# Attention weights times normalised rows first, then times the value weights, with row sums from the exponentials' accumulator

## The chip, the cores and the metric

One core of one Trainium2 chip runs the whole program. The metric is the device time of one execution in microseconds, as the median over several runs. The engines are called TensorE (PE; its weight loads PEld), VectorE (DVE), ScalarE (ACT), GpSimd (POOL) and SyncE (SP, which issues DMAs here).

## What is computed

The input is 16 batches of 64 channels x 250 samples; the output is 16 x 250 x 128. Cut to what matters:

```python
h = layernorm_affine(conv3(x).T @ lin_w.T + ...)       # tokeniser, per batch 250 x 128
n = layernorm(h)                                       # n1 in the kernel
QK = (n @ Wq) @ (n @ Wk).T                             # 250 x 250 per batch
c0 = argmin(sum(QK[0], axis=1))                        # one row, found in batch 0
A  = softmax(QK / 8); A[:, c0, :] = 0
h  = h + A @ (n @ Wv)                                  # the product whose order changes
h  = h + gelu(layernorm(h) @ tril(W1).T + b1) @ tril(W2).T + b2
```

All of it is float32.

## The kernel before

The 250 tokens of a batch lie as two interleaved halves (a = 0, 1) of 125 partitions. NB is 16 batches, NP is 8 pairs of batches. Five engine programs are written out by hand and meet only through semaphores; each engine runs its own list in order, so the written order decides what can stand behind what.

Per batch b, TensorE turns the normalised rows (turn_n1, L353), multiplies them with Wq Wk^T (queries, L358) and with Wv (values, L363), makes the scores (scores, L371), turns the exponentials (turn_a, L380) and multiplies them with the values (attend, L390). The values carry a 129th column of ones, so attend also gives the softmax's row sums. Per pair, project (L400, L403) makes the tokeniser's product. A float32 product is two instructions of TensorE; a transposition here is one.

ScalarE copies every result out of PSUM (out_n1t L563, out_p L567, out_v L572, out_at L585), normalises the rows for all but the first two batches (normalize_1, L556), takes the sums of squares (squares, L547, with the accumulator), and the exponentials (exps, L578: two ACTIVATEs, one for each half).

VectorE adds the taps of the convolution (L686, L693), scales (scale_x, L703), takes statistics (stats_1 L710, aggregate_1 L716, stats_2 L765, aggregate_2 L771), the row maxima (row_max, L746) and the residual (residual, L751 reciprocal of the row sums, L753 times keep, L757 the two updates of h). For the feed-forward part it normalises (normalize_2, L893: four TENSOR_SCALARs a pair) and adds the result (finish, L883).

GpSimd takes the roots (root_x L235, root_1 L249, root_2 L263), adds beta (add_beta, L267), the first tap (L224), and b2 (add_b2, L271).

The steady part is a hardware loop (Fori) on each engine: on TensorE `queries, values, project, turn_a, scores, turn_n1, attend` for the even batch, the same without project for the odd. VectorE's loop for the pair k is

```python
residual(2 * k - 2); stats_1(k + 1); second_tap(k + 3, x_slot); aggregate_1()
third_tap(k + 3, x_slot); row_max(2 * k, 0)
stats_2(k - 1, 0); residual(2 * k - 1); stats_2(k - 1, 1); scale_x(k + 2)
row_max(2 * k + 1, 1); aggregate_2()
```

Behind the loop the last three pairs are written out, and in them the first pairs of the feed-forward part begin: normalize_2(1, 1) stands between residual(12) and row_max(14), and GpSimd's order there is root_2(NP - 3), add_b2(0), add_b2(1), root_2(NP - 2), add_b2(2), root_2(NP - 1), then add_b2(3) to add_b2(7). ScalarE's order at the end is exps(15), out_at(15), gelu(0) with its table load, and so on.

## Time and profile before

| what | us |
|---|---|
| median of 3 runs | 112.07 |
| lowest and highest run | 110.67 to 112.18 |
| the profiled execution, device time | 111.78 |
| its span, first to last instruction | 109.9 |

The profile shows one execution, whose own device time is 1.9 us more than its span. Busy times are sums over the span; what an engine waited for is told in views of their own. Times inside the trace are counted from the start of the span.

### The profile page before, as it was taken

Reading aid. Unit: us, or ns where it says so; the run is one execution under the profiler, and the core shown is the slowest. Engines: PE = TensorE matmul, PEld = TensorE weight load, DVE = VectorE, ACT = ScalarE, POOL = GpSimd, SP = SyncE. Lnnn points to the kernel's source line nnn. Section 1 sums busy time; section 2 is a strip of 40 time slices with the busy share of each in tenths; the row PEclk is TensorE's granted clock in tenths of the full one; section 3 lists DMA queues with packets and bytes.
Section 4 is the critical chain, followed back from the end, with each engine's and each line's share of the span. In section 5 each row is a group of like instructions: output and inputs, shape, how many; then the busy total and the mean of one; then the engine's idle time right before and its main releaser. Section 6 shows DMA issues by size and latency. Waiting matters only on the chain.

```text
span 109.9 us, 2404 instructions
## 1 busy us (share of the span) xinstructions
PE 96.4 (88%) x618; PEld 76.3 (69%) x618; DVE 91.2 (83%) x335; ACT 67.9 (62%) x207; POOL 59.6 (54%) x122
## 2 busy tenths in 40 slices
PE   6976978989899999999999998999799786699930
PEld 2443465868778888888888997997686663486730
DVE  2679999999999889979979789999959999994250
ACT  3132445985668888887896989797476744226400
POOL 3327687548549649758758648509309069920000
PEclk9999999999999999999999999999999999769996
DMA  2960000000010010010000000000000003026363
GB/s 57 171 243 0 0 0 3 0 6 6 0 47 0 11 35 0 4 43 0 0 0 3 0 0 0 0 6 0 0 0 0 0 0 93 18 79 186 94 173 107
DMA packets 3838, 3.80 MB, mean 35 GB/s; under 512 B 426, under 2 KB 3703, under 8 KB 3831
## 3 DMA queue, kind: packets, MB, share of 16 engines
q1 hardware_dynamic: 3557, 3.40, 11.4%
q10 hardware_dynamic: 274, 0.33, 1.3%
q8 instruction: 2, 0.03, 0.1%
q14 instruction: 5, 0.04, 0.1%
HBM read 1.68 MB, written 2.05 MB: 34 GB/s over the span
## 4 chain that ended last, share of the span: by engine, by line
DVE 39%; PE 30%; POOL 10%; issue 9%; POOLq 3%; ACT 3%; DVEq 1%; ACTq 0%
DVE n L893 7%; PE bank_o L411 6%; DVE scaled L703 5%; PE bank_s L371 4%; DVE neg_max L746 4%; POOL rstd_x L235 4%; POOL rstd L249 4%; DVE h_all L757 3%; DVE bn L710 3%; DVE rinv_keep L753 3%; PE bank_s L497 2%; DVE bn L765 2%; DVE tap L686 2%; DVE mv L771 2%; PE bank_at L505 2%
## 5 line engine op out<-in xcount | busy, mean ns | idle before, releaser
L578 ACT ACTIVATE a<-bank_s,neg_max 125x250 f32<-125x250 f32 x32 | 13.3, 467 | 8.7 <-DVE neg_max L746 8.4
L390 PE MATMUL bank_o<-v,at 125*125 125x129 f32 x128 | 17.7, 280 | 0.0
L371 PE MATMUL bank_s<-n1t,pt 128*125 128x250 f32 x64 | 16.4, 379 | 0.6 <-ACT pt L567 0.6
L390 PEld LDWEIGHTS bank_o<-v,at 125*125 125x125 f32 x128 | 15.4, 187 | 1.7 <-ACT at L585 0.9
L893 DVE TENSOR_SCALAR n<-h_all,mean,rstd 125x128 f32<-125x128 f32 x32 | 16.0, 563 | 0.0
L746 DVE TENSOR_REDUCE neg_max<-bank_s 125x2 f32<-125x500 f32 x16 | 10.7, 671 | 2.1 <-PE bank_s L371 1.9
L556 ACT ACTIVATE n<-h_all,shift,rstd 125x128 f32 (+1 forms) x28 | 12.2, 488 | 0.3 <-POOL shift L254 0.3
L267 POOL TENSOR_TENSOR h_all<-scaled,rows_sb 125x512 f32<-125x512 f32 (+1 forms) x6 | 7.6, 1274 | 8.2 <-DVE scaled L703 8.2
L371 PEld LDWEIGHTS bank_s<-n1t,pt 128*125 128x125 f32 x64 | 10.7, 187 | 1.9 <-ACT pt L567 1.2
L380 PE MATMUL bank_at<-ident,a 125*125 125x125 f32 x64 | 10.5, 286 | 1.3 <-ACT a L578 1.3
L358 PE MATMUL bank_np<-n1t,qk_w 128*128 128x250 f32 x32 | 9.6, 382 | 1.4 <-ACT n1t L563 1.0
L757 DVE SCALAR_TENSOR_TENSOR h_all<-bank_o,rinv_keep,h_all 125x128 f32<-125x128 f32 (+1 forms) x32 | 9.8, 346 | 1.3 <-DVE rinv_keep L753 0.5
L380 PEld LDWEIGHTS bank_at<-ident,a 125*125 125x125 f32 x64 | 8.3, 188 | 2.7 <-ACT a L578 2.5
L547 ACT ACTIVATE squared<-bank_x 125x128 f32<-125x128 f32 x28 | 7.7, 298 | 3.8 <-PE bank_x L403 3.8
L271 POOL TENSOR_TENSOR hb_all<-h_all,rows_sb 125x512 f32 (+1 forms) x8 | 10.1, 1283 | 0.0
L585 ACT ACTIVATE at<-bank_at 125x500 f32<-125x500 f32 x16 | 9.5, 592 | 0.9 <-PE bank_at L380 0.9
L363 PEld LDWEIGHTS bank_v<-w_sb,n1t 128*125 128x125 f32 x64 | 9.5, 187 | 0.7
L235 POOL TENSOR_TENSOR rstd_x<-var_x_eps,neg_half 125x4 f32<-125x4 f32 (+1 forms) x10 | 9.1, 909 | 1.2
L363 PE MATMUL bank_v<-w_sb,n1t 128*125 128x128 f32 x64 | 9.6, 272 | 0.0
L646 ACT ACTIVATE n2t<-bank_x 128x500 f32<-128x500 f32 x8 | 4.7, 590 | 7.6 <-PE bank_x L490 7.5
L703 DVE SCALAR_TENSOR_TENSOR scaled<-bank_x,rstd_x,rows_sb 125x128 f32<-125x128 f32 x28 | 7.9, 343 | 1.3 <-POOL rstd_x L235 1.3
L249 POOL TENSOR_TENSOR rstd<-var_eps,neg_half 125x4 f32<-125x4 f32 (+1 forms) x10 | 8.8, 884 | 0.2
(111 smaller groups left out, 203.6 us busy)
## 6 DMA issues: line engine op xcount, KB each, us to landing
out_dram<-hb_all SPq DMA_DIRECT2D x7, 224.0 KB
x_head<-x_dram SPq DMA_DIRECT2D x4, 125.0 KB, 5.5
x_slot<-x_dram SPq DMA_DIRECT2D x4, 125.0 KB, 2.0
w_sb<-weights_dram SPq DMA_DIRECT2D x1, 320.5 KB, 5.7
out_dram<-hb_all SPq DMA_DIRECT2D x2, 112.0 KB
rows_sb<-rows_dram ACTq DMA_DIRECT2D x1, 187.5 KB
out_dram<-hb_all SPq DMA_DIRECT2D x7, 26.0 KB
tok_w<-tok_dram ACTq DMA_DIRECT2D x1, 130.0 KB, 2.7
```

Of the source, the lines that this page charges most:

```text
L235: pool.tensor_tensor(rstd_x[:, tiles], var_x_eps[:, tiles], neg_half[:, tiles], ALU.pow)\
L249: pool.tensor_tensor(rstd1[:, tiles], var1_eps[:, tiles], neg_half[:, tiles], ALU.pow)\
L363: last = nc.tensor.matmul(v_ps[:, a, :], n1t[par][:, a * H:(a + 1) * H], w_v, start=True, stop=True)
L371: last = nc.tensor.matmul(s_ps[par][:, a, :], pt[par][:, a * H:(a + 1) * H], n1t[par][:, :], start=True, stop=True)
L380: last = nc.tensor.transpose(at_ps[:, c, a * H:(a + 1) * H], a_sb[par][:, a, c * H:(c + 1) * H], ident[0:H, 0:H])
L390: last = nc.tensor.matmul(o_ps[:, a, 0:DV], at_sb[par][:, c, a * H:(a + 1) * H], v_sb[par][:, c, :], start=(c == 0), stop=(c == 1))
L556: last = nc.scalar.activation(n1[par][:, a, :], h_pairs[:, pair, n * D:(n + 1) * D], ACT.Identity, bias=shift1[:, n:n + 1], scale=rstd1[:, ...
L578: last = nc.scalar.activation(a_sb[par][:, a, :], s_ps[par][:, a, :], ACT.Exp, bias=neg_max[par][:, a:a + 1])
L703: last = nc.vector.scalar_tensor_tensor(scaled[:, n, :], src[n // 2][:, n % 2, :], rstd_x[:, n:n + 1], gamma, ALU.mult, ALU.mult)
L746: nc.vector.tensor_reduce(neg_max[par][:, :], s_ps[par], AX_X, ALU.max, negate=True).then_inc(max_ready, 1)
L757: last = nc.vector.scalar_tensor_tensor(h, o_ps[:, a, 0:D], rinv_keep[:, a:a + 1], h, ALU.mult, ALU.add)
L893: last = nc.vector.tensor_scalar(n2[par][:, n, :], h_pairs[:, j, n * D:(n + 1) * D], mean2[:, j, n:n + 1], rstd2[:, j, n:n + 1], ALU.subtr ...
```

## The change

The product A (n Wv) is made as (A n) Wv. TensorE no longer makes values. A new step, mix, multiplies the normalised rows of the batch (as weights, n1) with the turned exponentials, two products of 250 columns summed in PSUM; ScalarE copies the result out (out_mix), and attend multiplies it with Wv, two products of 128 columns. n1 gets four buffers instead of two. attend(b) moves to the step of the batch b + 2.

The row sums come from the accumulator of the exponentials (`accum_out`), into four columns for a pair. VectorE inverts them once a pair (inverse_sums), multiplies with keep once a pair (drop_row), and residual only updates h. The exponentials are written as two halves with out_mix of the batch before between them. VectorE's order changes: stats_1 and aggregate_1 stand ahead of residual(2k-2), scale_x ahead of residual(2k-1), and at the end normalize_2(1, 1) ahead of residual(12). The loops of TensorE, ScalarE and VectorE over the pairs are written out.

```diff
-            def values(b, par):
-                for a in range(2):
-                    last = nc.tensor.matmul(v_ps[:, a, :], n1t[par][:, a * H:(a + 1) * H], w_v,
-                                            start=True, stop=True)
-                last.then_inc(v_mm, 1)
+            def mix(b, par):
+                pe.wait_ge(at_ready, b + 1)
+                for c in range(2):
+                    last = nc.tensor.matmul(mix_ps, n1[b % 4][:, c, :], at_sb[par][:, c, :], start=(c == 0), stop=(c == 1))
+                last.then_inc(mix_mm, 1)
...
             def attend(b, par):
-                pe.wait_ge(at_ready, b + 1)
+                pe.wait_ge(mixed_ready, b + 1)
...
                 for a in range(2):
-                    for c in range(2):
-                        last = nc.tensor.matmul(o_ps[:, a, 0:DV], at_sb[par][:, c, a * H:(a + 1) * H],
-                                                v_sb[par][:, c, :], start=(c == 0), stop=(c == 1))
+                    last = nc.tensor.matmul(o_ps[:, a, :], mixed[par][:, a * H:(a + 1) * H], w_v, start=True, stop=True)
...
+            for b in range(2, NB - 1):
+                par = b % 2
+                queries(b, par)
+                if par == 0 and b // 2 + 2 < NP:
+                    pe.wait_ge(x_scaled, b + 4)
+                    project(b // 2 + 2)
+                if b == 2:
+                    pe.wait_ge(sums_used, 1)
+                attend(b - 2, par)
+                turn_a(b - 1, 1 - par)
+                scores(b, par)
+                turn_n1(b + 1)
+                mix(b - 1, 1 - par)
...
             queries(NB - 1, 1)
-            values(NB - 1, 1)
             turn_n2(0, 0)
+            attend(NB - 3, 1)
             turn_a(NB - 2, 0)
             scores(NB - 1, 1)
             turn_n2(1, 1)
-            attend(NB - 2, 0)
+            mix(NB - 2, 0)
             pe.wait_ge(tri_ready, 2)
             up(0, 0)
+            attend(NB - 2, 0)
             turn_a(NB - 1, 1)
             up(1, 1)
-            attend(NB - 1, 1)
+            mix(NB - 1, 1)
             turn_n2(2, 0)
             down(0, 0)
+            attend(NB - 1, 1)
...
+            def exps(b, par, halves=(0, 1)):
                 act.wait_ge(max_ready, b + 1)
-                for a in range(2):
+                for a in halves:
                     last = nc.scalar.activation(a_sb[par][:, a, :], s_ps[par][:, a, :], ACT.Exp,
-                                                bias=neg_max[par][:, a:a + 1])
-                last.then_inc(exp_ready, 1)
+                                                bias=neg_max[par][:, a:a + 1],
+                                                accum_out=exp_sum[:, 2 * par + a:2 * par + a + 1])
+                if 1 in halves:
+                    last.then_inc(exp_ready, 1)
...
+            def slot(b):
+                par = b % 2
+                xs = par == 0 and b // 2 + 2 < NP
+                out_p(b, par)
+                normalize_1((b + 1) // 2, 1 - par)
                 if xs:
...
+                out_at(b - 1, 1 - par)
...
+                out_n1t(b + 1, 1 - par)
+                exps(b, par, (0,))
+                out_mix(b - 1, 1 - par)
+                exps(b, par, (1,))
...
             out_p(NB - 1, 1)
-            out_v(NB - 1, 1)
             out_n2t(0, 0)
             out_at(NB - 2, 0)
             out_n2t(1, 1)
-            exps(NB - 1, 1)
+            exps(NB - 1, 1, (0,))
+            out_mix(NB - 2, 0)
+            exps(NB - 1, 1, (1,))
             out_at(NB - 1, 1)
             gelu(0, 0)
+            out_mix(NB - 1, 1)
...
-            def residual(b):
-                dve.wait_ge(o_mm, b + 1)
-                nc.vector.reciprocal(rinv[:, :], o_ps[:, :, D]).then_inc(rinv_ready, 1)
...
+            def inverse_sums(k):
+                dve.wait_ge(exp_ready, 2 * k + 2)
+                nc.vector.reciprocal(rinv[:, :], exp_sum[:, :]).then_inc(rinv_ready, 1)
+            def drop_row(k):
+                dve.wait_ge(rinv_ready, k + 1)
+                nc.vector.tensor_tensor(rinv_keep[:, :], rinv[:, :], keep[:, :], ALU.mult).then_inc(keep_applied, 1)
+            def residual(b, k, par):
+                dve.wait_ge(keep_applied, k + 1)
                 dve.wait_ge(o_mm, b + 1)
...
-            with dve.Fori(2, NP - 3) as k:
-                residual(2 * k - 2)
+            for k in range(2, NP - 3):
                 stats_1(k + 1)
+                inverse_sums(k - 1)
                 dve.wait_ge(bn1_ready, 2 * k + 4)
                 second_tap(k + 3, x_slot)
                 aggregate_1()
+                drop_row(k - 1)
+                residual(2 * k - 2, k - 1, 0)
                 third_tap(k + 3, x_slot)
                 row_max(2 * k, 0)
                 from_scores(k)
...
             for k in range(NP - 3, NP):
-                residual(2 * k - 2)
                 if k < NP - 1:
...
                 else:
+                    inverse_sums(k - 1)
                     normalize_2(1, 1)
+                drop_row(k - 1)
+                residual(2 * k - 2, k - 1, 0)
                 row_max(2 * k, 0)
...
-            residual(NB - 2)
+            normalize_2(2, 0)
+            inverse_sums(NP - 1)
+            drop_row(NP - 1)
+            residual(NB - 2, NP - 1, 0)
             stats_2(NP - 1, 0)
-            normalize_2(2, 0)
             normalize_2(3, 1)
-            residual(NB - 1)
+            residual(NB - 1, NP - 1, 1)
```

## Rows read from the trace of the kernel before

**Rows 1.** The page, part 1: busy time of each engine, share of the span, instructions.

```profile
PE 96.4 (88%) x618; PEld 76.3 (69%) x618; DVE 91.2 (83%) x335; ACT 67.9 (62%) x207; POOL 59.6 (54%) x122
```

**Rows 2.** The chain that ended last: start, duration, piece; one TensorE step, and one project.

```profile
19.31 0.43 PE bank_x L400 x4
19.74 0.26 PE bank_x L403 x2
...
69.35 0.89 PE bank_o L390 x8
70.24 0.42 PE bank_np L358 x2
70.66 0.44 PE bank_v L363 x4
71.10 0.44 PE bank_at L380 x4
71.53 0.86 PE bank_s L371 x4
```

**Rows 3.** Timeline (start, duration, engine, line, instruction, [idle before <-releaser]): row maxima of batches 2 and 13.

```profile
28.24 0.65 DVE L746 TENSOR_REDUCE neg_max<-bank_s 125x2 f32<-125x500 f32 x1
...
72.42 0.68 DVE L746 TENSOR_REDUCE neg_max<-bank_s 125x2 f32<-125x500 f32 x1
```

**Rows 4.** Timeline, VectorE and GpSimd over one pair of the loop (45 to 53 us).

```profile
44.73 0.37 DVE L716 BATCH_NORM_AGGREGATE mv<-bn 125x2 f32<-125x6 f32 x4
...
48.41 1.13 DVE L703 SCALAR_TENSOR_TENSOR scaled<-bank_x,rstd_x,rows_sb 125x128 f32<-125x128 f32 x4 [0.32 <-POOL rstd_x L235]
...
49.79 1.27 POOL L267 TENSOR_TENSOR h_all<-scaled,rows_sb 125x512 f32 x1 [1.41 <-DVE scaled L703]
...
50.50 0.57 DVE L753 TENSOR_TENSOR rinv_keep<-rinv,keep 125x2 f32<-125x2 f32 x1
...
52.75 0.48 DVE L686 SCALAR_TENSOR_TENSOR tap<-x_slot,tok_w,tap 128x250 f32<-128x250 f32 x1
...
53.14 0.37 DVE L716 BATCH_NORM_AGGREGATE mv<-bn 125x2 f32<-125x6 f32 x4
```

**Rows 5.** Timeline: ScalarE with and without the accumulator, and from exponentials to scores.

```profile
43.49 0.39 ACT L572 ACTIVATE v<-bank_v 125x256 f32<-125x256 f32 x1
...
43.75 0.29 ACT L547 ACTIVATE squared<-bank_x 125x128 f32<-125x128 f32 x1
...
43.91 0.22 ACT L547 ACTIVATION_READ_ACCUMULATOR squared<-bank_x 125x1 f32 x1
44.00 0.30 ACT L547 ACTIVATE squared<-bank_x 125x128 f32<-125x128 f32 x1
...
46.09 0.83 ACT L578 ACTIVATE a<-bank_s,neg_max 125x250 f32<-125x250 f32 x2 [0.44 <-DVE neg_max L746]
...
46.97 0.70 PE L380 MATMUL bank_at<-ident,a 125*125 125x125 f32 x4
...
47.51 1.01 PE L371 MATMUL bank_s<-n1t,pt 128*125 128x250 f32 x4
```

**Rows 6.** Timeline, VectorE and GpSimd: normalize_2(0, 0), normalize_2(1, 1), row_max(14).

```profile
71.20 1.11 DVE L893 TENSOR_SCALAR n<-h_all,mean,rstd 125x128 f32<-125x128 f32 x4
...
73.53 0.38 DVE L771 BATCH_NORM_AGGREGATE mv<-bn 125x2 f32<-125x6 f32 x4
...
74.75 3.09 DVE L893 TENSOR_SCALAR n<-h_all,mean,rstd 125x128 f32<-125x128 f32 x4
...
75.26 2.50 POOL L271 TENSOR_TENSOR hb_all<-h_all,rows_sb 125x512 f32<-125x512 f32 x2
...
77.77 0.67 DVE L746 TENSOR_REDUCE neg_max<-bank_s 125x2 f32<-125x500 f32 x1
```

**Rows 7.** Timeline of the last batch: table load of gelu(0), the last residual.

```profile
84.13 1.28 ACT L650 ACT_TABLE_LOAD   x1
...
87.25 0.61 DVE L757 SCALAR_TENSOR_TENSOR h_all<-bank_o,rinv_keep,h_all 125x128 f32<-125x128 f32 x2
```

More of the change, by code:

```diff
@@ L451, in _ @@
             scores(1, 1)
-            turn_n1(2, 0)
-            pe.wait_ge(v_ready, 2)
+            turn_n1(2)
             pe.wait_ge(sums_diagonal, 1)
             nc.tensor.matmul(sums_ps, ones_f[:, :], sum_diag[:, :], start=True, stop=True).then_inc(sums_spread, 1)
-            pe.wait_ge(v_ones, 2)
-            attend(0, 0)
-            pe.wait_ge(sums_used, 1)
-            with pe.Fori(1, NP - 2) as k:
-                queries(2 * k, 0)
-                values(2 * k, 0)
-                pe.wait_ge(x_scaled, 2 * k + 4)
-                project(k + 2)
-                turn_a(2 * k - 1, 1)
-                scores(2 * k, 0)
-                turn_n1(2 * k + 1, 1)
-                attend(2 * k - 1, 1)
-                queries(2 * k + 1, 1)
-                values(2 * k + 1, 1)
-                turn_a(2 * k, 0)
-                scores(2 * k + 1, 1)
-                turn_n1(2 * k + 2, 0)
-                attend(2 * k, 0)
-            for b in range(NB - 4, NB - 1):
-                queries(b, b % 2)
-                values(b, b % 2)
-                turn_a(b - 1, 1 - b % 2)
-                scores(b, b % 2)
-                turn_n1(b + 1, 1 - b % 2)
-                attend(b - 1, 1 - b % 2)
+            mix(0, 0)
+            for b in range(2, NB - 1):
[11 more added lines that the diff above has]
+                mix(b - 1, 1 - par)
             def turn_n2(j, par):
@@ L585, in out_at @@
                 nc.scalar.activation(at_sb[par][:, :, :], at_ps, ACT.Copy).then_inc(at_ready, 1)
[L587 to L591 removed]
+            def slot(b):
[3 more added lines that the diff above has]
+                normalize_1((b + 1) // 2, 1 - par)
                 if xs:
[L593 removed]
+                    act.wait_ge(x_mm, b + 6)
                     squares(0)
                     squares(1)
[L596 removed]
+                out_at(b - 1, 1 - par)
                 if xs:
@@ L636, in _ @@
             out_n1t(2, 0)
-            exps(1, 1)
-            with act.Fori(1, NP - 2) as k:
-                step(k)
-            step(NP - 2, xs=False)
+            exps(1, 1, (0,))
+            out_mix(0, 0)
+            exps(1, 1, (1,))
+            for b in range(2, NB - 1):
+                slot(b)
             def out_n2t(j, par):
@@ L650, in gelu @@
                 nc.scalar.activation(g_sb[par][:, :], f1_ps[par], ACT.Gelu, bias=b1_col).then_inc(gelu_ready, 1)
-            normalize_1(NP - 1, 1)
-            out_p(NB - 2, 0)
-            out_v(NB - 2, 0)
-            out_at(NB - 3, 1)
-            out_n1t(NB - 1, 1)
-            exps(NB - 2, 0)
             out_p(NB - 1, 1)
-            out_v(NB - 1, 1)
             out_n2t(0, 0)
@@ L848, in from_scores @@
                 stats_2(k - 1, 0)
-                residual(2 * k - 1)
+                scale_x(k + 2)
+                residual(2 * k - 1, k - 1, 1)
+                row_max(2 * k + 1, 1)
                 stats_2(k - 1, 1)
-                scale_x(k + 2)
                 dve.wait_ge(bn2_ready, 2 * k)
-                row_max(2 * k + 1, 1)
                 aggregate_2()
             dve.wait_ge(keep_ready, 1)
-            residual(0)
             stats_1(2)
+            inverse_sums(0)
             dve.wait_ge(bn1_ready, 6)
```

96 lines of the change are left out of this document (38 added, 58 removed).

## Prediction, made before the changed kernel was run

> **What bounds the kernel now.** I read the page first. TensorE is busy for 88% of the span and VectorE for 83%, ScalarE for 62% [rows 1]: two engines are near full, so a saving on one of them alone gives little, and an order that makes one wait for the other costs at once. Then I read the chain that ended last, which shows TensorE's instructions back to back where it is the bound [rows 2], and the timeline of one pair of the loop [rows 4]. From aggregate to aggregate a pair takes 8.41 us (44.73 to 53.14). Inside it lies a circuit of VectorE and GpSimd: aggregate_1, GpSimd's two roots, scale_x 3.68 us later, row_max, aggregate_2, residual, stats_1, second tap, aggregate_1 again. TensorE's own work for a pair is 2 x 3.27 + 1.38 = 7.92 us: a batch without project is attend 0.89, queries 0.42, values 0.44, turn_a 0.44, scores 0.86 and 0.22 for turn_n1 (two transpositions; four take 0.44), and project is 2 x (0.43 + 0.26) [rows 2]. So TensorE has only 0.5 us of slack in 8.41.
>
> The third view is the link between two batches: row_max, the exponentials, turn_a, the next scores. Today: scores 1.01 to their end, 0.04 to VectorE, row_max 0.67, 0.03, both exponentials 0.83, 0.05, and 0.54 from turn_a's start to the start of scores [rows 3, 5], together 3.17 us. TensorE's work for a batch is 3.27, so this link is hidden with 0.1 to spare. It is the number on which the change turns.
>
> **TensorE's work.** values (0.44) and attend (0.89) go. mix is two products of 250 columns, the shape of scores: 0.86. The new attend is two products of 128 columns, the shape of values: 0.44. Sum 1.30 against 1.33: TensorE saves 0.03 us a batch, 0.5 us in all, and only where it is the bound. That the new order of the product saves columns on paper is nearly undone, since the old one has 128 and 129 columns per product and the new one 250. A batch now takes 3.24, a pair 7.86.
>
> **ScalarE's work and the link.** out_v (256 columns, 0.26 from its start to the next start) is replaced by out_mix (250 columns), at the same price. New are the reads of the accumulator. At squares the read starts 0.16 after its ACTIVATE and the next instruction 0.09 after the read; the read lasts 0.22 [rows 5]. An exponential alone takes 0.47, and the second starts 0.36 after the first (0.83 less 0.47). With reads and out_mix between the halves the link holds: 0.36 + 0.09 for the first half, 0.28 for out_mix, then 0.35 + 0.22 for the second with its read: 1.30 us instead of 0.83. From below it could be 0.83 + 0.09 = 0.92 (out_mix costs nothing, reads overlap, and the semaphore goes with the ACTIVATE); from above it is more if mix isn't ready. It should be just ready: after scores begin, turn_n1 and mix follow at 0.86 and 1.08, mix ends at about 2.1, and the first exponential's half is done at 1.01 + 0.04 + 0.67 + 0.03 + 0.45 = 2.2. I take 1.30, the sum of the nearest rows. The link becomes 3.17 + 0.47 = 3.64 us. TensorE has 3.24 of work to cover it in an odd step and 4.62 in a step with project. So an odd step becomes 3.64 long and a pair 4.63 + 3.64 = 8.27 us, against 8.41 today.
>
> **VectorE's circuit.** A pair loses one reciprocal and one multiplication by keep. That multiplication lasts 0.57 us on the loop's path, though it has two columns: it ends when GpSimd's add_beta (49.79 + 1.27 = 51.06) ends [rows 4]. drop_row now stands behind aggregate_1, where GpSimd waits for it, so it costs 0.16 there. With scale_x, residual, row_max, stats_2, aggregate_2, stats_1, reciprocal, second tap (0.39 to its follower) one after another, each by the distance of its start to its follower's on the timeline, I get 3.68 + 1.05 + 0.54 + 0.58 + 0.50 + 0.29 + 0.79 + 0.20 + 0.40 = 8.03. That is shorter than 8.27; so VectorE's gain of 0.38 a pair is real but cut to 0.14 by the link. Written-out loops: TensorE's back edge shows at most 0.1 us, inside the slack; I give it nothing of its own.
>
> **Head.** row_max(2) starts at 28.24 [rows 3]. Before it now stand both taps of x_slot (0.40 each by their starts), less the first reciprocal and its wait (0.2): 28.84. The values of the first two batches lay beside ScalarE's copies and give nothing.
>
> **Through the pairs.** row_max(10) comes four pairs later: 28.84 + 33.08 = 61.92. From there no project covers the link; row_max(13) = 61.92 + 3 x 3.64 = 72.84 (now 72.42 [rows 3]): +0.42.
>
> **normalize_2(1, 1) and the port.** Now: aggregate_2 at 73.53, four TENSOR_SCALARs from 74.75 take 3.09 us, alongside two add_b2 from 75.26 for 2.50, and row_max(14) starts at 77.77 [rows 6]. Alone a group of four takes 1.11 (71.20); so two of the four each sat through one add of 1.27. In the new order aggregate_2 is at 73.95, and inverse_sums(6) must wait for the exponentials of batch 13: 72.84 + 0.67 + 0.04 + 1.30 = 74.85. The four instructions start at 75.07, 75.34, 75.61 and 75.88; add_b2(0) comes as now 1.73 after aggregate_2, at 75.68. So only the fourth is caught (until 77.03); but then drop_row, two inputs in SBUF, is caught by add_b2(1) until 78.2, as the 0.57 row shows for its two-column form. residual 0.54, row_max(14) at 78.8: +1.05. If drop_row slipped through, it would be 77.7. What is queued behind drop_row is the residual, then row_max(14), then everything on TensorE.
>
> The Trainium skill, page "SBUF — State Buffer", section "Who interferes with whom", says the same of drop_row: a VectorE instruction with two SBUF inputs contends with a GpSimd instruction that reads SBUF, and whoever issues first holds the port for the whole instruction. By that rule the trace agrees (0.57 us for two columns), and by that page alone the sum would be this one and not the 77.7.
>
> **Last batch.** Now the last residual starts 9.48 after row_max(14) [rows 6, 7]. New, from row_max(14) = R: exponentials done R + 2.01; turn_a, scores(15), row_max(15) at R + 3.65; exponentials with out_mix(14) done R + 5.8. TensorE: mix(14) and up(0) to R + 5.59, attend(14) to 6.03, turn_a(15) to 6.6, out_at(15) to 7.25. Then the table load of 1.28 [rows 7] and gelu(0) 0.68 end at R + 9.25, and out_mix(15) stands behind them: 9.6. down(0) 0.87 starts at 9.28, so attend(15) ends at R + 10.75 and the residual comes at R + 10.8: +1.32. Today attend(15) has no copy behind the table load; this is what the new copy costs. aggregate_2 and the rest of the tail wait for it in VectorE's order.
>
> **Sum.** 0.42 + 0.63 + 1.32 = 2.4 us. The profiled execution took 111.78 (span 109.9 and 1.9 around it), so 114.2; it lies 0.3 under the median of the runs, 112.07, which is inside their spread, so I leave it. Against the median that is +1.9%; about 2% is what a measurement of this kernel can tell from no change.
>
> **Rivals.**
> *The link stays hidden (faster).* If the exponentials' link is 0.92 and not 1.30, VectorE's 8.03 rules: row_max(10) at 60.96, then 3.27 a batch: row_max(13) at 70.8. normalize_2(1, 1) then starts 0.7 after aggregate_2 and escapes the adds, drop_row sits through one: row_max(14) at 75.5, 2.3 early; the tail costs about 0.6. Time 110.1, and under 109.8 (2%) if drop_row is free too. For it: out_mix might fit in idle time (ScalarE waits 0.44 us for the row maximum). Against: it stands behind the row maximum in ScalarE's list, not ahead. It decides where the link is under 1.0 us. Chance 0.17.
> *mix is late (slower).* If mix isn't ready when the first half is done, the second half, turn_a and scores wait. I left 0.1 us. out_at stands behind out_p and normalize_1 in ScalarE's list, and the copy lasts 0.6. If each odd step and each step without project loses 0.3 more, that is nine steps, 2.7 us: 116.9. It decides from 0.1 us of delay on. Chance 0.2.
> *The port misses drop_row, or the tail has slack.* R 1.1 earlier, or attend(15) released earlier: 112.3 to 113.2. Chance 0.15.
> *The change does what the forecast says.* Chance 0.48.
>
> The range from these: 110.8 to 116.6 leaves out part of the first two. The likeliest case's own range is 113.2 to 115.2. Faster by over 2%: 0.12; within 2% (109.8 to 114.3): 0.48; slower: 0.40, half of it from the forecast's own upper side.
>
> **What would show it.** Right: row_max of odd and even batches 3.6 and 4.6 us apart in the loop; 1.3 us from the first exponential to turn_a; a wait of turn_a for the exponentials in nearly every odd step; drop_row of over 1 us near 77 us; attend(15) behind gelu(0) and out_mix. Wrong: a pair of 8.0 (the link is hidden), of over 8.5 (mix late, second exponentials waiting for mix), row_max(14) before 77.7, or pauses of no known cause in the written-out loops.

## The result and the profile after

The changed kernel takes 113.43 us (median of 5 runs, 112.69 to 117.67), the kernel before 111.76 in the runs beside it: ratio 1.0167, 95% interval 1.0109 to 1.0224. In a second measurement it was 113.69 against 112.30: 1.013 (1.0065 to 1.0195). So it is slower by 1.3 to 1.7%: both intervals lie above 1, and only the first reaches past 2%. 114.2 us had been forecast. (The ratios here are not the quotients of the medians; the two differ by up to 0.7 points.) In some executions the granted clock is low for longer and the time some per cent greater, and the first profile of the changed kernel was of such a one, so all rows below are from the second profile, of the same kernel (span 111.9 us, device time 113.6).

The page of the changed kernel, part 1, the line that answers to [rows 1]:

```profile
PE 94.1 (84%) x554; PEld 71.1 (64%) x554; DVE 85.8 (77%) x319; ACT 71.1 (64%) x239; POOL 60.0 (54%) x120
```

TensorE is busy for 2.3 us less and VectorE for 5.4 less; ScalarE has 3.2 more, and the kernel is slower. Busy time is not even a measure of the work: before, TensorE counts as busy through the whole 8.41 us of a pair, while its products, each by the distance to its follower, add up to 7.92. So busy time doesn't tell it; the waits do. The timeline of the changed kernel over one odd step, from row_max(10) to row_max(11) (start, duration, engine, line, instruction, [idle before <-releaser]):

```profile
62.30 0.68 DVE L724 TENSOR_REDUCE neg_max<-bank_s 125x2 f32<-125x500 f32 x1 [0.60 <-PE bank_s L369]
...
63.01 0.47 ACT L562 ACTIVATE a<-bank_s,neg_max 125x250 f32<-125x250 f32 x1
...
63.38 0.19 ACT L562 ACTIVATION_READ_ACCUMULATOR a<-bank_s,neg_max 125x1 f32 x1
63.47 0.37 ACT L556 ACTIVATE mixed<-bank_m 128x250 f32<-128x250 f32 x1
63.73 0.47 ACT L562 ACTIVATE a<-bank_s,neg_max 125x250 f32<-125x250 f32 x1
...
63.89 0.51 PEld L387 LDWEIGHTS bank_o<-w_sb,mixed 128*125 128x125 f32 x4 [0.54 <-ACT mixed L556]
64.08 0.21 ACT L562 ACTIVATION_READ_ACCUMULATOR a<-bank_s,neg_max 125x1 f32 x1
...
64.43 0.61 PE L378 MATMUL bank_at<-ident,a 125*125 125x125 f32 x4
...
64.88 1.01 PE L369 MATMUL bank_s<-n1t,pt 128*125 128x250 f32 x4
...
65.93 0.68 DVE L724 TENSOR_REDUCE neg_max<-bank_s 125x2 f32<-125x500 f32 x1 [0.20 <-PE bank_s L369]
```

The step is 3.63 us. In it the exponentials, both accumulator reads and out_mix between them last from 63.01 to 64.29, 1.28 us, where both exponentials took 0.83 in [rows 5]. TensorE's weight loads for attend now wait 0.54 us for out_mix, and its products start at 63.89, 0.3 us later than back to back behind the queries; in [rows 2] there is no such gap.

The timeline of the changed kernel at row_max(14), which answers to [rows 6]:

```profile
73.19 0.68 DVE L724 TENSOR_REDUCE neg_max<-bank_s 125x2 f32<-125x500 f32 x1 [0.61 <-PE bank_s L369]
...
75.21 0.18 DVE L729 RECIPROCAL rinv<-exp_sum 125x4 f32<-125x4 f32 x1 [0.54 <-ACT a L562]
...
75.31 2.08 DVE L881 TENSOR_SCALAR n<-h_all,mean,rstd 125x128 f32<-125x128 f32 x4
...
76.03 2.50 POOL L271 TENSOR_TENSOR hb_all<-h_all,rows_sb 125x512 f32<-125x512 f32 x2
...
77.30 1.25 DVE L733 TENSOR_TENSOR rinv_keep<-rinv,keep 125x4 f32<-125x4 f32 x1
...
78.58 0.61 DVE L741 SCALAR_TENSOR_TENSOR h_all<-bank_o,rinv_keep,h_all 125x128 f32<-125x128 f32 x2
79.11 0.67 DVE L724 TENSOR_REDUCE neg_max<-bank_s 125x2 f32<-125x500 f32 x1
```

drop_row, four columns wide, takes 1.25 us: it ends when the second addition of b2 ends. And the last batch, which answers to [rows 7]:

```profile
86.32 1.28 ACT L632 ACT_TABLE_LOAD   x1
...
87.62 0.68 ACT L632 ACTIVATE g<-bank_s,w_sb 128x500 f32<-128x500 f32 x1
88.19 0.37 ACT L556 ACTIVATE mixed<-bank_m 128x250 f32<-128x250 f32 x1
...
89.32 0.60 PE L387 MATMUL bank_o<-w_sb,mixed 128*125 128x128 f32 x4
...
90.03 0.61 DVE L741 SCALAR_TENSOR_TENSOR h_all<-bank_o,rinv_keep,h_all 125x128 f32<-125x128 f32 x2 [2.10 <-PE bank_o L387]
```

Where the two profiled executions part, in us (the end is that of the last addition to the output, finish):

| stretch | before | changed | difference | forecast |
|---|---|---|---|---|
| start to row_max(0) | 16.92 | 17.45 | +0.53 | 0 |
| row_max(0) to row_max(2) | 11.32 | 11.73 | +0.41 | +0.60 |
| row_max(2) to row_max(13) | 44.18 | 44.01 | -0.17 | -0.18 |
| row_max(13) to row_max(14) | 5.35 | 5.92 | +0.57 | +0.63 |
| row_max(14) to the last residual | 9.48 | 10.92 | +1.44 | +1.32 |
| last residual to the end | 18.73 | 17.95 | -0.78 | 0 |
| sum | | | +2.00 | +2.37 |

### The profile page after: what moved, and what is told of

It reads as the page before. It is cut to its first block, busy times and chain, and to the rows that moved or that the text cites. A ratio compares the mean times of both kernels' runs of the same rounds, so it can differ in the third digit from the quotient of the medians.

```text
span 116.0 us, 2145 instructions
## 1 busy us (share of the span) xinstructions
PE 99.3 (86%) x554; PEld 74.3 (64%) x554; DVE 86.0 (74%) x319; ACT 71.1 (61%) x239; POOL 59.9 (52%) x120
## 4 chain that ended last, share of the span: by engine, by line
PE 56%; DVE 14%; ACT 12%; DMA 5%; issue 4%; POOLq 2%; POOL 1%; SPq 1%; DVEq 0%; ACTq 0%
PE bank_s L369 12%; PE bank_o L387 8%; PE bank_at L378 6%; DMA w_sb<-weights_dram 5%; ACT a L562 5%; PE bank_x L396 5%; PE bank_m L362 5%; PE bank_o L407 5%; DVE neg_max L724 5%; DVE n L881 5%; PE bank_np L356 3%; PE bank_x L399 3%; PE bank_s L478 3%; PE bank_np L486 3%; ACT mixed L556 2%
## 5 line engine op out<-in xcount | busy, mean ns | idle before, releaser
L562 ACT ACTIVATE a<-bank_s,neg_max 125x250 f32<-125x250 f32 x32 | 15.0, 469 | 3.7 <-DVE neg_max L724 2.4
L362 PE MATMUL bank_m<-at,n 125*128 125x250 f32 x64 | 16.9, 388 | 0.0
L724 DVE TENSOR_REDUCE neg_max<-bank_s 125x2 f32<-125x500 f32 x16 | 10.8, 678 | 7.9 <-PE bank_s L369 7.7
L741 DVE SCALAR_TENSOR_TENSOR h_all<-bank_o,rinv_keep,h_all 125x128 f32<-125x128 f32 x32 | 9.7, 345 | 6.1 <-PE bank_o L387 6.0
L881 DVE TENSOR_SCALAR n<-h_all,mean,rstd 125x128 f32<-125x128 f32 x32 | 14.1, 502 | 0.0
L387 PE MATMUL bank_o<-w_sb,mixed 128*125 128x128 f32 x64 | 10.9, 294 | 3.0 <-ACT mixed L556 2.0
L387 PEld LDWEIGHTS bank_o<-w_sb,mixed 128*125 128x125 f32 x64 | 8.3, 188 | 6.9 <-ACT mixed L556 6.9
L362 PEld LDWEIGHTS bank_m<-at,n 125*128 125x128 f32 x64 | 11.5, 199 | 1.5 <-ACT at L571 0.6
L540 ACT ACTIVATE n<-h_all,shift,rstd 125x128 f32<-125x128 f32 x28 | 12.4, 504 | 0.0
L407 PE MATMUL bank_o<-warm 128*64 128x512 bf16 x24 | 10.1, 587 | 1.0 <-DVE warm L759 1.0
L547 ACT ACTIVATE n1t<-bank_np 128x250 f32<-128x250 f32 x16 | 6.1, 382 | 7.9 <-PE bank_np L351 7.9
```

Of the source, the lines that this page charges most:

```text
L362: last = nc.tensor.matmul(mix_ps, n1[b % 4][:, c, :], at_sb[par][:, c, :], start=(c == 0), stop=(c == 1))
L387: last = nc.tensor.matmul(o_ps[:, a, :], mixed[par][:, a * H:(a + 1) * H], w_v, start=True, stop=True)
L407: nc.tensor.matmul(bank_o[0:64, :], warm[:, :], warm[:, :].unsqueeze(1).broadcast_to((128, 8, 64)), start=True, stop=True)
L540: last = nc.scalar.activation(n1[b % 4][:, a, :], h_pairs[:, pair, n * D:(n + 1) * D], ACT.Identity, bias=shift1[:, n:n + 1], scale=rstd1[ ...
L562: last = nc.scalar.activation(a_sb[par][:, a, :], s_ps[par][:, a, :], ACT.Exp, bias=neg_max[par][:, a:a + 1], accum_out=exp_sum[:, 2 * par ...
L724: nc.vector.tensor_reduce(neg_max[par][:, :], s_ps[par], AX_X, ALU.max, negate=True).then_inc(max_ready, 1)
```

## The experiments

Theory: the link through the exponentials sets the odd steps, one for one; the port costs one addition at row_max(14); out_mix(15) behind gelu(0) costs the last residual 1.3 us. The rival for each: the cost is hidden elsewhere and the loss comes from something else. The comparisons of the changed kernel run again, of no accumulator reads, of the copy made twice and of row_max(14) first share their runs of before (median 112.30); the next four kernels in this section share theirs (111.57), the three after them theirs (111.56), and the last has its own (112.38).

**The changed kernel once more.**

> The changed kernel as it is. The profile on record has TensorE's granted clock at half for parts of its first 30 us and again near 84 us; this run is to give rows of an undisturbed execution and a tighter ratio. Both theories: ratio 1.010 to 1.022. The link theory (from the row maximum to the exponentials' end, then turn_a, then the next scores) expects row maxima 3.63 us apart in odd steps and 4.65 in even ones; the rival, that the wider product mix or its TensorE time is the cost, expects odd steps where TensorE does not wait at turn_a.

It gave the rows above and the second ratio, 1.013. The steps are as expected, 3.63 and 4.65, but the wait shows mostly at attend and not at turn_a.

**No accumulator reads.**

```diff
                     last = nc.scalar.activation(a_sb[par][:, a, :], s_ps[par][:, a, :], ACT.Exp,
-                                                bias=neg_max[par][:, a:a + 1],
-                                                accum_out=exp_sum[:, 2 * par + a:2 * par + a + 1])
+                                                bias=neg_max[par][:, a:a + 1])
```

> The changed kernel without the accumulator in the exponentials; the row sums are left out (ones in their place), so h is not scaled by them. The link theory: each half loses its read (0.09 between the halves, 0.10 at the end), the odd steps go from 3.63 to 3.44 us, and over four pairs, three single batches and the last one the time falls by 9 x 0.19 = 1.7 us, to a ratio of 1.001 against the kernel before. The rival (TensorE's work or the order of VectorE binds): under 0.4 us.

Measured 111.72 us, ratio 0.997 (0.9916 to 1.0024), 1.6% below the changed kernel. That is about the gain that was expected (ratio 1.001), but less than half of it comes from where it was expected. The odd step is 3.53 instead of 3.63, a gain of 0.10 where 0.19 had been taken out of the link:

```profile
62.09 0.47 ACT L562 ACTIVATE a<-bank_s,neg_max 125x250 f32<-125x250 f32 x1
62.26 0.51 PEld L387 LDWEIGHTS bank_o<-w_sb,mixed 128*125 128x125 f32 x4 [0.44 <-ACT mixed L556]
...
62.69 0.52 PEld L378 LDWEIGHTS bank_at<-ident,a 125*125 125x125 f32 x4
```

The exponentials end at 62.56, and turn_a's weights follow at 62.69, behind attend. So the read between the halves counts, since it delays out_mix and with it attend by 0.09; the read behind the second half is covered by attend. Over four pairs, three single steps and the last batch that is 0.9 us. The larger part of the gain is elsewhere, in the timeline at row_max(14):

```profile
73.27 1.11 DVE L881 TENSOR_SCALAR n<-h_all,mean,rstd 125x128 f32<-125x128 f32 x4
...
74.17 2.56 POOL L271 TENSOR_TENSOR hb_all<-h_all,rows_sb 125x512 f32<-125x512 f32 x2
74.29 1.23 DVE L732 TENSOR_TENSOR rinv_keep<-rinv,keep 125x4 f32<-125x4 f32 x1
```

Here the group of four starts 1.94 us after row_max(13) (71.33), in the changed kernel 2.12 (75.31 less 73.19). The additions come 2.84 after row_max(13) in both. So a start 0.18 us earlier lets the fourth TENSOR_SCALAR through ahead of them, only drop_row is caught, and row_max(14) comes 4.75 after row_max(13) instead of 5.92: 1.17 us, about one addition, for two reads of 0.09.

**The copy out of mix made twice.**

```diff
                 act.wait_ge(mix_mm, b + 1)
+                nc.scalar.activation(mixed_twice[:, :], mix_ps, ACT.Copy)
                 nc.scalar.activation(mixed[par][:, :], mix_ps, ACT.Copy).then_inc(mixed_ready, 1)
```

> The changed kernel with out_mix done twice (the first copy goes to a spare tile). It lengthens ScalarE's stretch between the two halves of the exponentials by one copy of 250 columns, 0.26 to 0.28 us, and touches nothing on TensorE or VectorE. The link theory: one to one, odd steps 3.90 us, row maxima of a pair 8.54 instead of 8.27, 10 x 0.27 = 2.7 us in all (ratio 1.040). The rival (ScalarE has slack): under 0.5 us.

Measured 117.67 us, ratio 1.0544 (1.0461 to 1.0627). The odd step is 3.89 (3.63 + 0.26, the distance from one copy to the next), the even 4.65 as before, the pair 8.55: the link passes on what is put in ahead of out_mix's end, one for one. The time is over the expectation, though, by 0.9 us in the medians (112.30 times 1.040 is 116.8) and by 1.6 in the ratio. It lies between row_max(14) and row_max(15): 5.39 us, where this kernel's other single steps take 3.89 to 3.90 (in the changed kernel it is 3.62). Windows of this kernel there (start:end, length, busy time of each engine, granted clock, DMA):

```profile
79.00:82.00 3.00, 0.90 (x7) 0.57 (x5) 2.20 (x7) 1.12 (x5) 0.46 (x1) 1.00 0.00 0
82.00:86.00 4.00, 3.97 (x17) 3.53 (x18) 1.04 (x3) 1.76 (x5) 0.00 (x0) 0.57 0.00 0
```

TensorE works 0.90 of the 3 us to 82, waiting for out_mix(13), which waits for row_max(14). Then the granted clock is at its lower level, 1.2 GHz, from 82.3 to 85.7, and TensorE is busy all the time. The step takes 1.5 us more than the others of this kernel (5.39 less 3.89).

**row_max(14) ahead of normalize_2(1, 1).** In the changed kernel:

```diff
                     inverse_sums(k - 1)
-                    normalize_2(1, 1)
                 drop_row(k - 1)
                 residual(2 * k - 2, k - 1, 0)
                 row_max(2 * k, 0)
+                if k == NP - 1:
+                    normalize_2(1, 1)
```

> The changed kernel with normalize_2(1, 1) behind row_max(14) instead of ahead of drop_row. The port theory: drop_row runs at about 0.9 us after aggregate_2(5)'s start and ahead of add_b2(0), so it takes 0.13 instead of 1.24 us; row_max(14) comes as soon as scores(14) is done, 3.65 after row_max(13) instead of 5.9, and 2.0 to 2.3 us are gained, of which the next row maximum may give back some tenths while normalize_2(1, 1) shares the port with add_b2: ratio 0.998. The rival (the tail waits for something else, the adds on GpSimd or the last batch's copies): under 0.7 us.

Measured 111.26 us, ratio 0.9912 (0.9871 to 0.9953), 2.2% under the changed kernel: more than expected. The timeline:

```profile
75.37 0.16 DVE L733 TENSOR_TENSOR rinv_keep<-rinv,keep 125x4 f32<-125x4 f32 x1
...
76.76 0.68 DVE L724 TENSOR_REDUCE neg_max<-bank_s 125x2 f32<-125x500 f32 x1 [0.58 <-PE bank_s L369]
77.35 1.98 DVE L881 TENSOR_SCALAR n<-h_all,mean,rstd 125x128 f32<-125x128 f32 x4
```

drop_row takes 0.16 instead of 1.25, row_max(14) comes 3.63 after row_max(13), as any odd step, and the TENSOR_SCALARs lose one addition where TensorE doesn't wait for it. The Trainium skill, page "SBUF — State Buffer", section "Who interferes with whom", says that VectorE and GpSimd share a port that the first to issue holds for a whole instruction, and that a VectorE instruction with two SBUF inputs contends for it with a GpSimd instruction that reads SBUF. The trace agrees: the same instruction takes 1.25 us beside an addition and 0.16 without one.

**The loops of the kernel before, written out, nothing else.**

> The kernel before with nothing changed but the loops of TensorE, ScalarE and VectorE over the pairs written out. The prediction gave this nothing: ratio 0.997 to 1.003, the pair still 8.4 us. A rival, that the hardware loops' registers and branches cost time at each wait on the circuit of VectorE and GpSimd (gaps of about 0.1 to 0.2 us ahead of aggregate_1 in the loop), expects the pair at 8.1 to 8.2 and about 1 us in all (0.991).

Measured 111.35 us, ratio 0.9993 (0.9934 to 1.0051). In the trace row_max(0) to row_max(14) is 60.16 us instead of 60.85, with 4.13 and 4.03 to 4.07 for a step in the middle instead of 4.33 and 4.04 to 4.08. A pair is 8.19 us where it was 8.41: that is what the rival expected (8.1 to 8.2), and not the 8.4 of the prediction, which gave the loops nothing. So the written-out loops save about 0.7 us in that execution; the medians can't tell this from nothing, and their interval allows it. In the changed kernel the pair is set by the link, and nothing of this shows.

**out_mix(15) ahead of gelu(0).** On top of the kernel with row_max(14) first:

```diff
             mix(NB - 1, 1)
             turn_n2(2, 0)
-            down(0, 0)
             attend(NB - 1, 1)
+            down(0, 0)
...
             out_at(NB - 1, 1)
-            gelu(0, 0)
             out_mix(NB - 1, 1)
+            gelu(0, 0)
```

> e4 with out_mix(15) ahead of gelu(0) on ScalarE and attend(15) ahead of down(0) on TensorE. The prediction's step on the last batch: the table load of 1.28 and gelu(0) no longer stand between mix(15) and attend(15), the last residual comes 1.4 us earlier, gelu(0) 0.4 later; the tail follows the residual, so 1.0 to 1.4 us less than e4, ratio 0.980. The rival (the tail waits for gelu and down, not for the last residual): no gain or a small loss.

Measured 109.74 us, ratio 0.985 (0.9776 to 0.9924). The timeline:

```profile
84.27 0.38 ACT L556 ACTIVATE mixed<-bank_m 128x250 f32<-128x250 f32 x1 [1.20 <-PE bank_m L362]
84.67 1.28 ACT L632 ACT_TABLE_LOAD   x1
...
85.51 0.61 DVE L741 SCALAR_TENSOR_TENSOR h_all<-bank_o,rinv_keep,h_all 125x128 f32<-125x128 f32 x2 [0.82 <-PE bank_o L387]
```

The last residual comes 9.67 after row_max(14) (75.84), in the kernel that this one starts from 10.95: 1.28 us, and 1.06 of it reach the end.

**The kernel before with row_max(14) first.** The same move of normalize_2(1, 1) as above, in the kernel before.

> The kernel before with normalize_2(1, 1) behind row_max(14). The port theory holds for it as well: row_max(14) starts at the end of scores(14), 76.1 instead of 77.8 us, and normalize_2(1, 1) shares the port with add_b2 while nothing waits for it: 1.2 to 1.7 us less, ratio 0.987. The rival (the stall is covered by what comes later): under 0.4 us.

Measured 110.49 us, ratio 0.9917 (0.9846 to 0.9988). So the wait at the port was there before the change. row_max(13) to row_max(14) shrinks by 1.58 us (5.35 to 3.77), but row_max(14) to row_max(15) grows by 0.51 and 1.08 are left at the last residual.

**Values first, with the rest of the change.** The product is A (n Wv) again, made from TensorE's and ScalarE's lists of the kernel before, written out; the row sums come from the accumulator, and VectorE's order is the changed one, with row_max(14) first.

```diff
+                                                accum_out=exp_sum[:, 2 * par + a:2 * par + a + 1])
...
-            with dve.Fori(2, NP - 3) as k:
-                residual(2 * k - 2)
+            for k in range(2, NP - 3):
                 stats_1(k + 1)
+                inverse_sums(k - 1)
...
+                drop_row(k - 1)
+                residual(2 * k - 2, k - 1, 0)
```

> Everything of the changed kernel but the order of the product: sums from the exponentials' accumulator, inverse_sums and drop_row once a pair, VectorE's new order, loops written out, normalize_2(1, 1) behind row_max(14) as in e4, and the values made first as in the kernel before (attend without the column of ones, no out_mix, attend(b) in the step of b + 1). The link theory: from the exponentials' start to their end 1.00 us instead of 1.29, odd steps 3.36, a pair 8.0, and at the end no copy of ScalarE stands between gelu(0) and attend(15): about 1.0 us over the pairs, 0.8 over the single batches, 1.3 at the end, so 108.2 us or a ratio of 0.966. The rival (the order of the product is not what costs): within 0.5 us of e4, 0.99.

Measured 109.73 us, ratio 0.9859 (0.9793 to 0.9924): a gain, but two points less than expected. The odd step is 3.36, the even one 4.95 where 4.65 was expected. The timeline:

```profile
56.72 1.13 DVE L701 SCALAR_TENSOR_TENSOR scaled<-bank_x,rstd_x,rows_sb 125x128 f32<-125x128 f32 x4 [0.74 <-POOL rstd_x L235]
57.76 0.60 DVE L761 SCALAR_TENSOR_TENSOR h_all<-bank_o,rinv_keep,h_all 125x128 f32<-125x128 f32 x2
...
58.28 0.67 DVE L744 TENSOR_REDUCE neg_max<-bank_s 125x2 f32<-125x500 f32 x1
...
58.51 1.11 PE L388 MATMUL bank_o<-v,at 125*125 125x128 f32 x8
```

attend writes bank_o, of which there is one, and must wait until the residual of the batch before has read it. That residual stands behind scale_x, which waits 0.74 for GpSimd's root. It ends at 58.36, and attend starts at 58.51; row_max (58.28) isn't held up by it, since the scores end only at 58.24. The gain expected in the single steps is missing too: row_max(10) to row_max(14) takes 14.63 us, in the changed order with row_max(14) first 14.52.

**The same with residual(2k-1) ahead of scale_x.**

```diff
                 stats_2(k - 1, 0)
-                scale_x(k + 2)
                 residual(2 * k - 1, k - 1, 1)
+                scale_x(k + 2)
```

> e6 with residual(2k-1) ahead of scale_x(k+2). In e6 the even steps took 4.95 us instead of 4.65: VectorE wrote residual(2k-1) only behind scale_x, and attend(2k), which shares the one bank of PSUM with attend(2k-1), waited for it on TensorE (start 0.14 us after the residual's end). If that is what held e6 back, the even steps go to 4.65, a pair to 8.0, and 4 x 0.3 = 1.2 us are gained: ratio 0.975. The rival (something else stretches the even step, such as values ahead of project): no change, 0.986.

Measured 108.2 us, ratio 0.9741 (0.9666 to 0.9817), as expected: the even step is 4.67, the pair 8.03, and the wait of scale_x now has the residual in it. The even steps without project still take 3.95 us, because scores wait there for out_p, which stands behind normalize_1 in ScalarE's list:

```profile
65.85 0.87 ACT L553 ACTIVATE n<-h_all,shift,rstd 125x128 f32<-125x128 f32 x2
...
66.62 0.37 ACT L564 ACTIVATE pt<-bank_np 128x250 f32<-128x250 f32 x1
...
67.04 1.11 PE L369 MATMUL bank_s<-n1t,pt 128*125 128x250 f32 x4 [0.33 <-ACT pt L564]
```

**mix behind both exponentials, in the changed order of the product.** From the kernel with both places mended, ratio 0.985. out_mix comes after the second exponential, in the steps without project attend moves behind scores, and residual moves behind the row maximum (this last not in the cut):

```diff
-                exps(b, par, (0,))
+                exps(b, par)
                 out_mix(b - 1, 1 - par)
-                exps(b, par, (1,))
...
-                attend(b - 2, par)
+                covered = par == 0 and b // 2 + 2 < NP
+                if covered:
+                    attend(b - 2, par)
                 turn_a(b - 1, 1 - par)
                 scores(b, par)
                 turn_n1(b + 1)
+                if not covered:
+                    attend(b - 2, par)
                 mix(b - 1, 1 - par)
```

> e7 (the changed product order with normalize_2(1, 1) behind row_max(14) and out_mix(15) ahead of gelu(0)) with out_mix behind both halves of the exponentials, and, where no project covers it, attend(b-2) behind scores(b) and residual behind the row maximum. The link theory: the copy leaves the link, exponentials to their end 1.00 instead of 1.29, odd steps 3.37, a pair 8.0 to 8.05 instead of 8.27, 4 x 0.25 + 5 x 0.25 = 2.2 us: ratio 0.966 against e7's 0.985. The rival (the copy or attend waits elsewhere in the step and costs the same): within 0.5 us of e7.

Measured 111.54 us, ratio 0.9979 (0.9933 to 1.0025): a miss, and slower than what it started from. The odd step fell only to 3.47 (3.37 expected), and the even one rose to 5.07, where TensorE has no slack. Its timeline, from an odd step and from the even one behind it:

```profile
46.80 0.38 ACT L560 ACTIVATE mixed<-bank_m 128x250 f32<-128x250 f32 x1
...
47.06 0.39 ACT L555 ACTIVATE pt<-bank_np 128x250 f32<-128x250 f32 x1
...
47.50 0.71 PEld L369 LDWEIGHTS bank_s<-n1t,pt 128*125 128x125 f32 x4
...
48.77 0.49 PE L387 MATMUL bank_o<-w_sb,mixed 128*125 128x128 f32 x3
...
51.75 0.65 PE L387 MATMUL bank_o<-w_sb,mixed 128*125 128x128 f32 x4
```

Two attends, 0.44 us each, now stand in the step that has project and one less in the step that had the wait: the expected pair of 8.0 leaves the moved attend out of the step it entered, though 4.62 and 0.44 is 5.06. In the odd step out_mix now delays out_p (47.06 to 47.45), for which the scores' weights wait until 47.50, 0.54 behind those of turn_a (46.96) instead of 0.43: the copy still costs 0.1 there, in another place.

**Additions of b2 earlier.** Values first, residual first, and GpSimd makes five additions at once ahead of root_2(6), so that fewer lie in the tail:

```diff
             root_2(NP - 3)
-            add_b2(0)
-            add_b2(1)
+            for k in range(5):
+                add_b2(k)
             root_2(NP - 2)
-            add_b2(2)
+            add_b2(5)
...
```

> e9 with GpSimd's add_b2(2) to add_b2(4) ahead of root_2(6) and add_b2(5) between root_2(6) and root_2(7), instead of five additions behind root_2(7). The port theory: behind root_2(7) the TENSOR_SCALARs of normalize_2(5) and (6) sat through about six additions (4.0 and 2.5 us instead of 1.1 each); with two additions left they sit through two or three, and 2.5 to 3.5 us of the tail go: ratio 0.948. The rival (the tail is TensorE's, 2.15 us a pair for four pairs, or the output's DMAs): under 1 us.

Measured 109.77 us, ratio 0.9838 (0.9764 to 0.9912): a miss by 3.6 points. The timeline:

```profile
75.29 6.17 POOL L271 TENSOR_TENSOR hb_all<-h_all,rows_sb 125x512 f32<-125x512 f32 x5
...
76.99 4.55 DVE L901 TENSOR_SCALAR n<-h_all,mean,rstd 125x128 f32<-125x128 f32 x4
...
81.60 0.65 PE L487 MATMUL bank_x<-ident,n 125*128 125x125 f32 x4 [1.57 <-DVE n L901]
...
82.59 1.46 PE L388 MATMUL bank_o<-v,at 125*125 125x128 f32 x8 [0.35 <-DVE h_all L761]
```

The last residual to the end did shrink, 17.95 to 16.09. But each of the four TENSOR_SCALARs of normalize_2(1, 1) sat through one addition, and row_max(15), behind it, came 5.97 after row_max(14) instead of 3.66. TensorE waited, and from 83.2 to 86.6 its granted clock was at the lower level.

**The same additions in the gap.** VectorE idles 1.18 us ahead of row_max(14); there goes normalize_2(1, 1), and GpSimd waits for it before it adds.

```diff
             root_2(NP - 3)
-            add_b2(0)
-            add_b2(1)
+            pool.wait_ge(n2_ready, 2)
+            for k in range(4):
+                add_b2(k)
             root_2(NP - 2)
-            add_b2(2)
+            add_b2(4)
...
                 residual(2 * k - 2, k - 1, 0)
-                row_max(2 * k, 0)
                 if k == NP - 1:
                     normalize_2(1, 1)
+                row_max(2 * k, 0)
```

> The kernel that makes the values first and updates h before scaling (e9), with the additions of b2 moved once more. In e9 VectorE is idle from 74.32 to 75.50 us, ahead of row_max(14); here normalize_2(1, 1) fills that gap instead of standing behind row_max(14) (the root it needs ends at 74.42, four TENSOR_SCALARs alone take 1.1 us: until 75.5). GpSimd waits for them and then makes add_b2(0) to add_b2(3) at 75.5 to 80.5, where VectorE has no TENSOR_SCALAR or TENSOR_TENSOR, since aggregate_2(6), which root_2(6) waits for, comes at 80.27. Behind root_2(7) stand three additions (3.8 us) instead of five (6.3). Theory 1, the tail waits for VectorE, whose TENSOR_SCALARs sit through the additions: row_max(14) and row_max(15) stay at about 75.6 and 79.2, four TENSOR_SCALARs that take 4.01 us in the tail of e9 take about 1.5 to 2.7, and the end comes 1.2 to 1.9 us earlier: ratio to the kernel before about 0.96. Theory 2, the tail is TensorE's and the additions only fill idle time of VectorE: the end as in e9, ratio 0.974. In no case should TensorE be idle for long around row_max(15), as it was in e10, where normalize_2(1, 1) itself sat through the additions.

Measured 106.92 us against 112.38, ratio 0.9563 (0.945 to 0.9675): the fastest of all, 1.3 us under the median of the kernel that it starts from (by the ratios 2.0, but its runs of before are 0.8 us slower than that kernel's). The timeline:

```profile
75.02 1.11 DVE L902 TENSOR_SCALAR n<-h_all,mean,rstd 125x128 f32<-125x128 f32 x4
76.28 0.68 DVE L745 TENSOR_REDUCE neg_max<-bank_s 125x2 f32<-125x500 f32 x1 [0.15 <-PE bank_s L370]
...
88.12 4.00 DVE L902 TENSOR_SCALAR n<-h_all,mean,rstd 125x128 f32<-125x128 f32 x4
...
92.65 1.10 DVE L902 TENSOR_SCALAR n<-h_all,mean,rstd 125x128 f32<-125x128 f32 x4
...
98.97 0.69 DVE L892 TENSOR_TENSOR hb_all<-bank_at,hb_all 125x512 f32<-125x512 f32 x1 [1.45 <-PE bank_at L503]
```

row_max(15) and the last residual come 3.67 and 8.79 after row_max(14), as without the edit (3.66 and 8.78), and the last residual to the end is 17.04 instead of 17.95. In the profiles the gain of 0.91 is less than the 1.2 to 1.9 expected, since the group that begins beside the additions still takes 4.00: three of them are enough to catch it. It is the next group that is free, 1.10 instead of 2.45. After it VectorE waits for TensorE, so there both theories hold in turn: VectorE's tail while the additions run, TensorE's behind them.

## Why the prediction was right

The direction, the size and the places of the loss came out. The head was sized too large, the start and the tail were left out, and the link came out partly by luck.

- **The link.** The terms [rows 3, 5] gave 1.30 us for the exponentials with what stands between; 1.28 was measured. The odd step is 3.63 (3.64), the even 4.65 (4.63), four pairs take 33.12 (33.08). The rival of the hidden link (under 1.0 us) is out; the doubled copy (+0.26 a step) shows that the step follows the link one for one in what stands ahead of out_mix's end.
- **mix late.** In the pairs and the single steps the second exponential starts 0.26 after out_mix, and out_mix doesn't wait for mix; this rival needed more than 0.1 us of delay, which didn't come.
- **What was not seen in it.** The wait was forecast at turn_a. It shows mostly at attend, for out_mix, a path that the sum doesn't have: attend's weights start at 63.89 and those of turn_a could follow 0.44 later, at 64.33; the second exponential with its read ends at 64.29, and turn_a's weights start at 64.34. Two waits end within 0.05 us of each other, so the sum of one gave the length of both, which is luck. The run without the reads shows that the paths are two: 0.19 us went from the one, and the step fell by 0.10. By this, taking out_mix from between the exponentials alone wouldn't have helped, since attend would wait longer for it (argued, not run); where attend was moved with it, it went into the step where TensorE is full.
- **VectorE's circuit.** The forecast that its gain is cut by the link holds: VectorE waits 0.60 and 0.20 for scores in the two steps. drop_row takes 0.13 in the loop (0.16 forecast).
- **The port.** That the fourth TENSOR_SCALAR and then drop_row each sit through one addition came as forecast: 5.92 us to row_max(14) against 5.98. With row_max(14) first, that stretch takes 3.63, 2.3 us less, and the medians differ by 2.4. It was right by a hair: a start 0.18 us earlier lets one of the two through.
- **The last batch.** The residual comes 10.92 after row_max(14), 10.8 were forecast, 9.48 before [rows 6, 7]. With out_mix(15) ahead of gelu(0) it comes 1.28 earlier, so it is the place of out_mix(15) behind the table load and gelu(0).
- **The head.** This term was too large: +0.60 forecast, +0.41 in the table, and +0.28 between two executions without a stretch of the lower clock in the head (11.60 in the kernel with out_mix(15) ahead of gelu(0), 11.32 before). Both taps do stand ahead of row_max(2), but the sum left the multiplication by keep as it was: from its start to its follower's it is 0.32 before, and drop_row's is 0.05.
- **The ends.** The forecast gave the start and the tail nothing, and the profiled executions differ there by +0.53 and -0.78. These are not the change. In the execution of before, the granted clock was at its lower level from 94.5 to 97.9, in the tail; its last residual to the end took 18.73, while eight kernels of this study without such a stretch there took 17.94 to 17.97 (18.2 in the two kernels with out_mix(15) ahead of gelu(0)). The execution of the changed kernel has its stretch at 7.6 to 11.0, in the head; row_max(0) starts at 17.40 to 17.71 in the six profiles that have one there (the first profile of the changed kernel, with several stretches, left out), and at 16.50 to 17.38 in those that don't. With both taken off, the trace differs by 2.0 - 0.53 + 0.78 = 2.25 us, and with the 0.13 of the head that also goes by the stretch it is 2.1; the forecast was 2.4, and the medians differ by 1.4 to 1.7.
- **The medians.** The single runs of the second measurement agree with 2.1: at a mean granted clock of 0.99 or more the changed kernel took 113.12 us and the kernel before 110.83 to 111.35 (four runs), 1.8 to 2.3 less. Against these runs the medians are 1.1 us higher for the kernel before (112.30 less 111.18, the mean of its four) and 0.6 for the changed one (113.69 less 113.12), so that part of the loss doesn't show in the medians; with one such run of the changed kernel this is an estimate. The forecast put its 2.4 on top of an execution that held such a stretch without saying so.

Windows of the kernel before over this stretch (columns as above):

```profile
91.00:94.00 3.00, 1.29 (x9) 0.87 (x8) 3.00 (x3) 0.95 (x2) 3.00 (x3) 1.00 0.31 88
94.00:98.00 4.00, 3.64 (x12) 2.65 (x13) 4.00 (x8) 1.26 (x2) 2.68 (x3) 0.57 0.22 64
```

What the parts are worth, taken together: two edits that leave the order of the product as it is (row_max(14) first, out_mix(15) ahead of gelu(0)) bring the changed kernel from 1.013 to 0.985. With values first, out_mix isn't in the link and the odd step is 3.36 instead of 3.63; once residual(2k-1) stands ahead of scale_x, the same row sums give 0.974. So the new order of the product is the part that the change pays with: TensorE's full step is as long either way (4.65 with mix, 4.67 with values), and the result must pass ScalarE in the middle of the link, or ahead of out_p, where it costs too. Between those two kernels, values first gains 1.0 us in the four pairs (32.11 against 33.11) and 0.9 in the last batch; in the four single steps it gains nothing (14.62 against 14.51), since its even ones wait for out_p. The changed product was not run with residual(2k-1) ahead of scale_x; its even step is already as long as TensorE's own work (4.65), so that nothing is to be had there, but this is argued and not shown. How much of the 0.974 is the row sums' and how much the written-out loops' is not told apart either.

## What to carry to other kernels

Where the time of a step is a chain through several engines, price a change by what it puts into that chain and not by the busy time that it takes away: 0.45 us put into the link of each odd step left 0.13 of the 0.38 us that VectorE's circuit saves in a pair by the prediction's sum. When an instruction is moved, add it to the step that it enters. Where two engines share a port, a group of small instructions in front of a wait belongs in an idle gap that ends before the other engine's long instructions begin, with a semaphore that holds the long instructions back until it is through.

## What the runs showed of the hardware

- **The port is handed over once per instruction.** When GpSimd has additions of 1.27 us queued, VectorE gets one TENSOR_SCALAR through for each: four take 4.00 us beside three additions and 4.01 beside five, against 1.1 alone, and 4.55 where each of the four sat through one. VectorE's instructions that read PSUM kept their time beside the additions: in the last kernel row_max took 0.68 us and the two updates of residual 0.61.
- **The granted clock falls in the middle of a run, for 3.4 us.** It went from 2.4 to 1.2 GHz after TensorE had waited 2.08 us in the tail of the kernel before, 2.13 us with the copy made twice, and 1.57 and 0.35 us with the additions early. It did not fall after waits of 1.99 us and, in the tail, of 2.1 us in the changed kernel, so the length of the wait alone doesn't decide it. The cost of one stretch was 0.8 us in the tail of the kernel before and 1.5 us in the attention of the kernel with two copies, where TensorE was the bound. In the head it came in six profiles, of kernels of both orders (between 7.6 and 11.6). What else decides is open.
- **The accumulator read costs the next instruction 0.09 us**, at the exponentials (250 columns) as at the squares (128 columns), though it lasts 0.19 to 0.23.
